# The next image's chain three units earlier in a group norm, channel attention and deformable convolution kernel

## The reference

```
def _gn(v, G=32): ...                          # group norm, 32 groups, no affine
def _L0(x):                                    # channel attention, per image
    qkv = w_qkv @ x;  attn = softmax(q @ k.T * SCALE)      # 192 x 192
    return w_out @ (attn @ v) + b_out
def _L1(x):                                    # deformable 3 x 3 convolution
    offset = clip(conv(x, off_w) + off_b, -8, 8)           # 18 channels
    mask = 2 * sigmoid(conv(x, mask_w) + mask_b)           # 9 channels
    y = deform_conv(x, offset, mask, proj_w) + proj_b      # bilinear sampling
    y = (y - mean) * rsqrt(var + 1e-5)  # mean, var over all images and pixels
    return gelu(y * gamma + beta)
x = x + _L0(_gn(x))
x = x + _L1(_gn(x))
```

## Time and profile before

| | |
|---|---|
| median of 3 runs | 3922.26 us (3920.33 to 3923.71) |
| profiled execution | 3912.95 us, span 3911.1 us |
| PE busy | 3499.2 us, 89% |
| weight loads (PEld) busy | 3042.3 us, 78% |
| DVE busy | 2563.2 us, 66% |
| ACT busy | 2123.8 us, 54% |
| POOL busy | 1479.6 us, 38% |
| granted TensorE clock, mean | 0.966 |
| load of x, issue to landing | 5.4 and 6.0 us |

### The profile page before, as it was taken

The page is one execution under the profiler, slowest core; times in us unless marked ns, Lnnn a source line. Parts: engine busy times, 40 slices in busy tenths (PEclk is TensorE's granted clock), DMA queues, the critical chain, the costliest instruction groups (busy, mean ns, idle before and its releaser), DMA issues.

```text
span 3911.1 us, 108686 instructions
## 1 busy us (share of the span) xinstructions
PE 3499.2 (89%) x38307; PEld 3042.3 (78%) x38307; DVE 2563.2 (66%) x5805; ACT 2123.8 (54%) x4790; POOL 1479.6 (38%) x1165
## 2 busy tenths in 40 slices
PE   3999999999999999999999999999999999999600
PEld 2788888888888888888888888888888888888600
DVE  3567766676677667666776676677666666776522
ACT  1556555565555555555555555555555655555422
POOL 1334433343444333434433343444343434443311
PEclk8999999999999999999999999999999999999855
DMA  2000010000001011100100010010001000110399
GB/s 65 20 10 29 29 29 21 29 29 27 12 29 29 22 29 29 29 10 29 29 29 21 29 29 29 11 29 29 21 29 29 29 15 23 29 29 10 108 363 320
DMA packets 50710, 169.91 MB, mean 43 GB/s; under 512 B 9664, under 2 KB 10880, under 8 KB 50176
## 3 DMA queue, kind: packets, MB, share of 16 engines
q1 hardware_dynamic: 39584, 136.75, 11.6%
q0 software_dynamic: 7168, 25.17, 1.6%
q10 hardware_dynamic: 3424, 0.90, 0.1%
HBM read 87.29 MB, written 75.50 MB: 42 GB/s over the span
## 4 chain that ended last, share of the span: by engine, by line
issue 37%; PE 36%; POOL 15%; DMA 4%; DVE 4%; ACT 2%; DVEq 1%; ACTq 1%; SPq 1%; POOLq 1%
POOL sT L1341 14%; PE sps L690 7%; PE acc L707 4%; PE acc L709 4%; PE acc L708 4%; DMA xn<-x_scratch 2%; PE zps L676 2%; PE zps L680 2%; PE zps L677 2%; PE zps L678 2%; PE zps L679 2%; DMA out<-x 1%; PE l L563 1%; DVE stats L994 1%; PE l L619 1%
## 5 line engine op out<-in xcount | busy, mean ns | idle before, releaser
L1341 POOL TENSOR_TENSOR sT<-ay,bx 128x768 f32<-128x768 f32 x768 | 1216.6, 1596 | 1037.1 <-PE sps L690 812.9
L1165 DVE TENSOR_TENSOR sl<-sps,sh 128x384 f16<-128x384 f32 x1536 | 847.1, 552 | 523.9 <-ACT sh L909 512.5
L707 PE MATMUL acc<-zh,sh 128*128 128x192 f16 x4608 | 1133.9, 246 | 0.3 <-ACT ypm L930 0.3
L709 PE MATMUL acc<-zh,sl 128*128 128x192 f16 x4608 | 1133.9, 246 | 0.0
L708 PE MATMUL acc<-zl,sh 128*128 128x192 f16 x4608 | 1133.9, 246 | 0.0
L909 ACT CAST sh<-sps 128x384 f16<-128x384 f32 x1536 | 737.7, 480 | 589.1 <-PE sps L690 579.8
L882 ACT CAST zh<-zps 128x288 f16<-128x288 f32 x1536 | 616.1, 401 | 694.0 <-PE zps L680 664.4
L1159 DVE TENSOR_TENSOR zl<-zps,zh 128x288 f16<-128x288 f32 x1536 | 696.0, 453 | 382.8 <-ACT zh L882 375.7
L690 PE MATMUL sps<-eye,sT 128*128 128x128 f32 x4608 | 773.6, 277 | 70.1 <-POOL sT L1341 64.6
L690 PEld LDWEIGHTS sps<-eye,sT 128*128 128x128 f32 x4608 | 541.6, 141 | 170.8 <-issue 114.2
L708 PEld LDWEIGHTS acc<-zl,sh 128*128 128x128 f16 x4608 | 451.0, 98 | 17.3
(11 more groups left out here) (202 smaller groups left out, 6366.8 us busy)
## 6 DMA issues: line engine op xcount, KB each, us to landing
xin<-in_x SPq DMA_DIRECT2D x32, 512.0 KB, 5.4
xin<-in_x SPq DMA_DIRECT2D x64, 256.0 KB, 6.0
x_scratch<-x SPq DMA_DIRECT2D x32, 512.0 KB, 2.7
y_scratch<-ych SPq DMA_DIRECT2D x32, 512.0 KB, 2.7
zh<-y_scratch SPq DMA_DIRECT2D x20, 512.0 KB, 10.6
zl<-x_scratch SPq DMA_DIRECT2D x20, 512.0 KB, 11.9
out<-zh POOLq DMA_DIRECT2D x20, 512.0 KB, 9.1
x_scratch<-x SPq DMA_DIRECT2D x32, 256.0 KB, 3.4
```

Source lines behind the costliest of these rows:

```text
L707: pe.matmul(acc[:, 0:C], s_h, zh[:, j, ky, z], start=start and kx == 0, stop=False)
L709: mm = pe.matmul(acc[:, 0:C], s_l, zh[:, j, ky, z], start=False, stop=stop and kx == 2)
L1165: dve.tensor_tensor(one(sl), sps[u % S_BANKS][:, 0:3 * P], one(sh), ALU.subtract).then_inc(s_lo, 1)
L1341: pool.tensor_tensor(sT[:, p % ST_RING].rearrange("p k (r x) -> p k r x", r=R), a, x_, ALU.mult)\
```

## The change

The slots of `part0` are called three units earlier: unit u now calls slot u + 3 (`LEAD`). Slots 0 to 2 would fall outside; they held the statistics of x, which DVE now takes in units 44 to 47 of the image before (for image 1: between the first image's chain and its convolution). The moments move to slot 3. From slot 28 on every slot number of the chain rises by one, so that those steps come two units earlier. POOL calls slots 2p - 3 and 2p - 2 behind product p, so its calls keep their place among the products up to slot 5, and slots 30 and 42 are called behind products 16 and 22, as 29 and 41 were. `turn_y` moves from units 29, 30, 37 to 26, 27, 36; the last one of an image (in unit 1 of the next) uses the other PSUM bank, and the wait that guarded the first group sums moves to the second transpose of x. The statistics of y move by a few units. Column hats, the copy of `acc` and the offset distance stay in their units. SyncE raises `x_loaded` once more behind the last load, for the statistics of an image that isn't there. DVE's slots 28, 32 to 36, 40, 41, 42, 44 and 46 each become one higher, like the ACT ones shown.

```diff
-        yt = [l0[1], l0[0], l0[0], l0[0]]
+        yt = [l0[1], l0[0], l0[0], l0[1]]
+        LEAD = 3
@@ images(), all engines @@
             for u in range(SLOTS):
                 part0(u, 0, 0)
+            stats_of_next()
             part1(0, 0, True)
@@ turns_y @@
-            return {29: 0, 30: 1, 37: 2}.get(u)
+            return {26: 0, 27: 1, 36: 2}.get(u)
@@ SyncE @@
             attended(NB - 1, False)
+            sp.sem_inc(x_loaded, 48)
@@ PE @@
-            def group_stats(n, b, again):
-                if n == 0 and not again and (not isinstance(b, int) or b >= 2):
-                    pe.wait_ge(y_ch, 4 * (b - 1))
+            def group_stats(n, b):
...
+            def transpose_x(r, b, again):
+                if r == 1 and not again and (not isinstance(b, int) or b >= 2):
+                    pe.wait_ge(y_ch, 4 * (b - 1))
@@ PE part0 @@
-                if u == 28:
-                    group_stats(1, b, again)
-                if 38 <= u < 40:
+                if u == 29:
+                    group_stats(1, b)
+                if 39 <= u < 41:
@@ part1 of PE, ACT, DVE @@
-                    if more:
-                        part0(u, b + 1, 1 - par)
+                    if more and u + LEAD < SLOTS:
+                        part0(u + LEAD, b + 1, 1 - par)
@@ ACT part0: normalize x1 @@
-                if 30 <= u < 34:
+                if 31 <= u < 35:
@@ mask @@
-                if u == 41:
+                if u == 42:
@@ |ay|, relu @@
-                if u in (41, 45):
+                if u in (42, 46):
-                if u == 42:
+                if u == 43:
                     column_hats(0, b)
@@ DVE @@
+            def input_stats(q, b):
+                if q == 0:
+                    dve.wait_ge(x_loaded, 48 * b + 48)
+                channel_stats(q, xin)
+
             def part0(u, b, par, again=False):
-                if u < 3:
-                    dve.wait_ge(x_loaded, 48 * b + 48)
-                    channel_stats(u, xin)
-                if u == 2:
-                    channel_stats(3, xin)
+                if u == 0 and (again or first(b)):
+                    dve.wait_ge(x_loaded, 48 * b + 96 if again else 48)
+                    for q in range(4):
+                        channel_stats(q, xin)
+                if u == 3:
                     channel_moments()
@@ DVE part1 @@
-                    if 5 <= u < 7 and not first(b):
-                        y_stats(u - 3, b - 1, 1 - par)
-                    if u in (37, 39):
-                        y_stats(u // 39, b, par)
+                    if u in (4, 6) and not first(b):
+                        y_stats(u // 2, b - 1, 1 - par)
+                    if u in (35, 36):
+                        y_stats(u - 35, b, par)
...
+                    if more and u >= UNITS - 4:
+                        input_stats(u - UNITS + 4, b + 2)
@@ POOL part0 @@
-                if u == 29:
+                if u == 30:
                     group_rstd(1, b)
-                if u == 41:
+                if u == 42:
                     column_distance(0, b, par)
...
-                        for u in (2 * p - 4, 2 * p - 3):
-                            part0(u, b + 1, 1 - par)
+                        for u in (2 * p - 6, 2 * p - 5):
+                            part0(u + LEAD, b + 1, 1 - par)
```

More of the change, by code:

```diff
@@ L340, in images @@
         def images(program, eng):
-            part0, part1, weights_ready = program
+            part0, part1, weights_ready, stats_of_next = program
             for u in range(SLOTS):
@@ L552, in square @@
                 mm.then_inc(done, 1)
-            def transpose_x(r, b):
+            def transpose_x(r, b, again):
+                if r == 1 and not again and (not isinstance(b, int) or b >= 2):
+                    pe.wait_ge(y_ch, 4 * (b - 1))
                 if r == 0:
@@ L631, in part0 @@
                 if u == 4:
-                    group_stats(0, b, again)
+                    group_stats(0, b)
                 if 12 <= u < 16:
-                    transpose_x(u - 12, b)
+                    transpose_x(u - 12, b, again)
                 if u == 16:
@@ L653, in part0 @@
                     apply_m(u - 23, b)
-                if u == 28:
-                    group_stats(1, b, again)
-                if 38 <= u < 40:
+                if u == 29:
+                    group_stats(1, b)
+                if 39 <= u < 41:
                     for t in range(TILES // 2):
-                        offset_conv(TILES // 2 * (u - 38) + t, b, par)
+                        offset_conv(TILES // 2 * (u - 39) + t, b, par)
             def z_group(g, b, par):
@@ L783, in _ @@
             wq, wk = wqk[:, :, 0:C], wqk[:, :, C:2 * C]
-            images((part0, part1, weights_ready), pe)
+            images((part0, part1, weights_ready, lambda: None), pe)
             if_far(pe, lambda: far_loop(pe, far_image), lambda: None)
@@ L851, in part0 @@
                     act.copy(mt_h[:, :, C:2 * P], mt[:, :, P:C]).then_inc(mt_hi, 1)
-                if 30 <= u < 34:
-                    if u == 30 and not again and (not isinstance(b, int) or b >= 2):
+                if 31 <= u < 35:
+                    if u == 31 and not again and (not isinstance(b, int) or b >= 2):
                         act.wait_ge(sz_done, UNITS * (b - 1))
-                    i = (u - 30) // 2
-                    normalize(u % 2, i, x1, inner(x2[2 * i], par), 1, b)
-                if u == 41:
+                    i = (u - 31) // 2
+                    normalize((u - 31) % 2, i, x1, inner(x2[2 * i], par), 1, b)
+                if u == 42:
                     act.wait_ge(off_sb, b + 1)
                     act.activation(mask[:, par], off[:, par, :, 2 * TAPS:J], ACT.Tanh, scale=0.5)
-                if u in (41, 45):
-                    h = u // 45
+                if u in (42, 46):
+                    h = u // 46
                     d = ay_half(h, par).rearrange("p t k n -> p (t k n)")
@@ L934, in part1 @@
                         split_z(u + AHEAD - UNITS, b + 1, 1 - par)
-                    if more:
-                        part0(u, b + 1, 1 - par)
-            images((part0, part1, lambda: None), act)
+                    if more and u + LEAD < SLOTS:
+                        part0(u + LEAD, b + 1, 1 - par)
+            images((part0, part1, lambda: None, lambda: None), act)
             if_far(act, lambda: far_loop(act, far_image), lambda: None)
@@ L1095, in part0 @@
                     channel_moments()
-                if u == 28:
+                if u == 29:
                     group_variance(1, b)
-                if u == 32:
+                if u == 33:
                     residue(0, inner(x2[1], par), inner(x2[0], par), 1, b)
-                if u == 33:
+                if u == 34:
                     if not first(b):
@@ L1103, in part0 @@
                     move(0, b, par)
-                if u == 34:
+                if u == 35:
                     residue(1, inner(x2[2], par)[CB:P], inner(x2[2], par)[CB:P], 1, b)
-                if u == 35:
+                if u == 36:
                     dve.wait_ge(xn_lo, 4 * b + 4)
                     move(1, b, par)
-                if u == 36:
+                if u == 37:
                     move(2, b, par).then_inc(x2_moved, 1)
-                if u == 40:
+                if u == 41:
                     dve.wait_ge(off_ps, b + 1)
@@ L1123, in part0 @@
                     dve.tensor_scalar(yx, yx, -MAX_OFF, MAX_OFF, ALU.max, ALU.min).then_inc(off_sb, 1)
-                if u in (41, 44):
-                    h = u // 44
+                if u in (42, 45):
+                    h = u // 45
                     dve.wait_ge(off_sb, b + 1)
@@ L1129, in part0 @@
                        .then_inc(dy_sb, 1)
-                if u in (42, 46):
-                    h = u // 46
+                if u in (43, 47):
+                    h = u // 47
                     dve.wait_ge(hat_act, 2 * b + h + 1)
@@ L1270, in part1 @@
                     y_stats(3, b, par)
-            images((part0, part1, weights_ready), dve)
+            images((part0, part1, weights_ready, lambda: [input_stats(q, 1) for q in range(4)]), dve)
             if_far(dve, lambda: far_loop(dve, far_image), lambda: None)
@@ L1345, in part1 @@
                     if more:
-                        for u in (2 * p - 4, 2 * p - 3):
-                            part0(u, b + 1, 1 - par)
-            images((part0, part1, lambda: None), pool)
+                        for u in (2 * p - 6, 2 * p - 5):
+                            part0(u + LEAD, b + 1, 1 - par)
+            images((part0, part1, lambda: None, lambda: None), pool)
             def far_image(b):
```

## The result

The changed kernel takes **4038.32 us** (median of 4 runs, 4036.69 to 4043.77) where the kernel before took 3921.30 in the same comparison: a ratio of 1.0303, 95% interval 1.0285 to 1.0321. It is slower by 117 us; forecast were 87. The profiled execution has a span of 4035.0 us (before: 3911.1) and a mean granted TensorE clock of 0.958 (before: 0.966).

The account below looks back on a forecast made before the run. TensorE's instruction stream and its waits were taken as the bound, 112.6 us per image. New losses 7.26 less old 4.57 gave 2.7 x 31 = 84, plus 2.5 once: 87 us more, median 4009 us, range 3930 to 4065.

Parts of the forecast that it names:

- 1, `mv`: End of unit 1: PE waits for mv from the moments now in unit 0; between 0 and 0.70, taken as 0.1 us.
- 6, `ypm`: Units 3 to 6: ACT's hats and two normalisations stand ahead of ypm, so PE gets acc late; loss 1.94 us.
- 18, `ypm`: Units 16 to 18: ACT's hats and exponentials share a unit ahead of ypm; 0.59 plus 0.08 at the probabilities, 0.67 us.
- 30, `ypm`: Units 28 to 30: ACT's hats and a normalisation stand ahead of ypm, so PE gets acc late; loss 0.9 us.
- 36, x2 copies: Units 30 to 36: late z split, and an x2 copy meeting an sT delays the offset convolution; 0.9 us (0.3 to 1.3).
- 42, `ypm`: Units 38 to 42: the chain behind the offset convolution now ends ahead of ypm of unit 41; loss 2.2 us.
- the old 4.57: Five PE waits per image, in units 4, 7, 28, 38 and 43, summing to 4.57 us, all expected to go.
- (1): Whole kernel: the old waits go and nothing takes their place; 139 us less, 2.5 more, 3786 us; chance 0.05.
- (2): Units 6 and 42: only the two large ypm losses hold, 4.14 against 4.57; about 3911 us; chance 0.12.
- (3): Units 5 to 12 and 30 to 37: DVE also becomes the bound, distance keeps 2.00 us; 4064 us; chance 0.15.
- (4): Unit 44: the change does not do what it says, for instance x not yet loaded; no size or chance given.
- The step that hung on the port: Unit 9: PE waits for DVE's second remainder behind the offset distance, shortened if POOL's product ends earlier; 0.55 us (0 to 1.44).

Follow-up runs that it names:

- experiment 2: The changed kernel with the next image's first column hats in slot 44 instead of 43, behind ypm of unit 41 on ACT: 3996.24 us.
- experiment 3: The changed kernel with column hats 1 to 3 in units 1, 13, 25 and the next image's first column hats in slot 44: 3932.02 us.
- experiment 5: The changed kernel with column hats 1 to 3 in units 1, 13, 25, first hats in slot 44, offset distance in unit 13 (last image 7): 3910.50 us.
- experiment 1: The changed kernel with ACT's column hats 1 to 3 in units 1, 13 and 25 instead of 4, 16 and 28: 3961.80 us.
- one half: The kernel before with only the statistics of x moved to units 44 to 47 of the preceding image: 3899.12 us, ratio 0.9955.

## Why the prediction was right, and what it lacked

**The mechanism was right.** What goes went: `sT` is out of PE's waits, the wait of z for x2 too, and `mv` is waited for only twice, the long one (14.2 us) ahead of the first image, and of the stalls of the earlier trace rows none is left. What comes came in its places. Forecast and measured (image 15, from the rows above; a start less the one ahead of it, less the normal spacing):

| unit | forecast | measured | shown by |
|---|---|---|---|
| 1, `mv` | 0.1 | 0 | unit 3.27 long = 1.68, `turn_y` 0.44 and the sums 1.15; 4.05 in experiments 2, 3 and 5 |
| 6, `ypm` | 1.94 | 1.92 | experiment 1: 0.63 left |
| 9, remainder | 0.55 | 0.58 | experiment 5: gone |
| 18, `ypm` | 0.67 | 0.56, and 0.10 at the probabilities | experiment 1: moves, does not go |
| 30, `ypm` | 0.9 | 0.91 | experiment 1: 0.5 left |
| 36, x2 copies | 0.9 | 0.80 | rows alone; nothing was run on it |
| 42, `ypm` | 2.2 | 2.20 | experiment 2: 0.89 left |
| sum | 7.26 | 7.07 | |

Less the old 4.57 this is 2.5 us per image, 78 us, where 2.7 and 84 stood. Of the rivals none holds: the waits did not simply go (1), the small terms were real (2), the distance did not keep its 2.00 us but took 1.28 (3), and DVE's statistics of x never waited for a load (4).

**The step that hung on the port.** For unit 9 the price lay between 0 and 1.44 and hung on whether `ypos` takes DVE 1.49 us or less once POOL's product ends earlier. Its source view after:

```profile
L1151 DVE TENSOR_SCALAR ypos<-off,cmid x32: 701/725/1100, 141.3 to 3741.0; 128x72 f32<-128x72 f32 x32
```

725 ns in the median, and not even that is the operation's own time: a product of POOL still runs beside it and ends 0.05 us ahead of it (started 0.81 us before `ypos`, 1.48 long). In experiment 5 the distance stands where no product runs, except in the last image:

```profile
L1151 DVE TENSOR_SCALAR ypos<-off,cmid x32: 248/249/1099, 151.8 to 3614.8; 128x72 f32<-128x72 f32 x32
```

0.25 us alone, so 1.24 of the 1.49 us and 0.48 of the 0.72 were waiting for POOL, in both cases until the product ended. The rule that I weighed there (the Trainium skill, "GPSIMD Engine Reference", section 1 "Specifications") agrees with the trace.

**What it lacked: the clock.** No term of the forecast asked what PE's clock does behind the stalls. It added the stalls up at full clock, 84 + 2.5, and there they cost 78 + 3.8. The profiled executions are 124 us apart, 37 more than the forecast: 36 us are the 21 stretches at half clock that the changed kernel has more, 1.3 came more ahead of the first image and 5 behind the last, and 6 less for the terms that came out smaller. (The medians are only 117 apart, as the profiled execution of the kernel before was 8 us below its median.) That the time fell so well inside the range is thus due to the range's room above, not to a term for the clock.

The trace of before held the question and a price. Its longest stall that comes in every image, 1.94 us, had no half clock behind it, but of the two at the turns of the loop, 2.47 and 2.32 us, the first had (the rows are in the section on the profile after), and the forecast put a stall of 2.2 in each image. Whether 2.2 is enough was not to be read from these two; as a possibility it belonged among the rivals, at up to 31 x 1.7 = 53 us. The Trainium skill, "TensorE: Matmul & The Clock Gate", part 1, says that the gate sets the clock by how busy the engine has been recently; that half clock stands right behind the long stalls, and never behind those of 1.31 and 1.83 us, agrees with that.

**What I misjudged afterwards** was the cover that a stall gives. The 2.2 us in unit 42 gave DVE time for the four stats: with it unit 1 takes 3.27 (the changed kernel, experiment 1), and once it was gone (experiment 2), `mv` was late by 0.78. The stall hid the next one, and the forecast's 0.1 for unit 1 was right only as long as it stood.

## What to carry to other kernels

Walk each engine in its own order around a single buffer that is freed on a schedule of its own: here everything that moved was cheap, the averages had ACT at 54%, and in all four losses at `ypm` a column-hat pair stood in front of one small copy. Before counting on the gain of one stall removed, ask which later operation lives on the time that it gives. When an order gives PE a regular stall that is longer than any regular one in the trace at hand, look what the clock does behind the rare long ones and price it as a case of its own; and try the parts of a change alone, since here one half gained 0.45% and the other half took it all back.

## What the runs showed that I had not expected

- Stalls of 2.2 us and more in a busy TensorE stream often have half clock behind them. It came behind none of the stalls of 1.31 and 1.83 us, behind none of those of 1.94 in the kernel before and of 1.92 in the changed one but behind 3 of 31 of the same unit 6 in experiment 2, behind 9 and 21 of 31 for stalls of 2.20 (experiment 1, the changed kernel), and behind 25 and 20 of 32 for 2.35 and 2.76 us. Each stretch is 3.4 us long and costs 1.7 us, nearly as much again as the stall. Why the same stall of 2.20 has it in 9 images of one kernel and 21 of another is open.
- A DVE operation that meets a product of POOL can be held until that product ends, and then its length says nothing of its own work: `ypos` takes 0.25 us alone, 0.72 and 1.49 beside a product. The forecast weighed this for `ypos` only. The scaling of the probabilities, which no step of it named, is held up in the same way: 1.00 us for a pair in experiment 1 instead of 0.54.
